# A transformer block on one core: square root on ScalarE, query projection ahead of the probabilities' transposes, band mask on small TensorE tiles

## The chip, the cores and the metric

The kernel runs on one core of a Trainium2 chip. The metric is the device time of one execution in microseconds (us). Shown are the median of several runs, and one further execution recorded by the hardware profiler. Engines: PE (TensorE, with PEld for its weight loads), DVE (VectorE), ACT (ScalarE), POOL (GpSimd), SP (queues the DMAs).

## The reference, cut to what matters

A time-mix block (RWKV style) comes first and a layer norm ends it; neither is touched. Between them lie six layers of local attention and a gated feed-forward block over 2048 tokens of 128 features, 16 heads of 64, a window of 32 and the window before it:

```
def l2norm(t): return t / max(norm(t, axis=-1), 1e-12)
q, k, v = split(shift_tokens(x) @ Wqkv, 3)          # 16 heads of 64
q = l2norm(q) * qs ; k = l2norm(k) * ksc            # then rotated by cos/sin tables
sim  = einsum(q, k of this window and the one before) * 8
sim  = where(i < j or i > j + w or no window before, -max, sim)
x = softmax(sim) @ v @ Wo + x
x = (a * gelu(gate)) @ W2 + b2 + x                  # a, gate = layernorm(shift_tokens(x)) @ W1 + b1
```

## The kernel before

Everything stays in SBUF in 32-bit floats; DMAs bring each layer's weights and spread the values `v` over window rows. The six layers of 16 token tiles (128 tokens) are 96 units of work in one software pipeline. In step `s` every engine works on several units at once: the projections and the norms of unit p = s+1, the rotated queries and keys, scores and softmax of unit a = s, and the mixing with the values and the output projection of unit b = s-1. The feed-forward part takes two tiles at a time, several steps later: odd steps hold its second half (GELU, `down`) and the start of the next norm, even steps hold `normed` and `widen`. A loop of 44 rounds, an odd step and an even step each, makes up most of the run.

The order on each engine is written out by hand in `step`, one copy per engine; engines meet only through semaphores (`wait_ge`). In the words of this document PE does in each step, in this order:

- p-transposes (L1270-1271): the probabilities of unit b, into `att`. They wait for the softmax (`weighed`) and for the last step's output in `att` having been added to the residual (`xb_ready`, DVE L1223).
- q projection (L1277-1280) into `proj_a`, k projection (L1291-1295) into `proj_b`, both of unit p.
- q-transposes of unit a (L1300, 1303), the mixing of unit b (L1308-1316, 64 products, each on a tile of 64 rows by 32 columns of the array), k-transposes of unit a (L1319-1321), o-transposes of unit b (L1323-1325).
- band and scores of unit a: two matmuls put the mask into the PSUM bank `turn` (L1331-1333), and 64 products on 64x32 tiles add the scores (L1334-1343).
- v projection of unit p (L1345-1351) into `proj_a`, once the normalized queries have been read from there (`united[0]`); in odd steps `down` and the centring of the next norm (L1354-1365), in even steps the norm's transposes (L1366-1373); the output projection of unit b (L1374-1381); in even steps `widen` (L1388-1392).

The norms of q and k: ACT squares both projections (L1054), DVE sums them (L1155), takes the root's inverse of 32 numbers per token in nine small instructions of its own (`inverse_root`, L82-105: a bit trick with `magic`, then two correction steps), and multiplies (`unite`, L1180). POOL then rotates q and k (L999, L1032, L1006; DVE does one of the products, L1233). The nine instructions hang on each other through the semaphore `rooted`. The DVE instructions ahead of them are the two halves of `divide_out` (L1161), which wait for the mixing.

ACT also copies PSUM to SBUF: `p_t`, `q_t`, `k_t`, `o_t`, `val` (the values). GELU, Exp and the other functions need table sets; a load (ACT_TABLE_LOAD) stands ahead of GELU in every odd step (L1068), and one ahead of a one-element Exp, `warm`, further down in the same step (L1093).

Of the kernel before, what the change touches and what calls it, by code (L numbers as in the profile page):

```python
# [37 lines left out]
WINDOW = 32  # L38
# [24 lines left out]
ROOT_SCALE = 3 / 8  # L63
# [15 lines left out]
ROOT_OPS = 9  # L79


def inverse_root(dve, ops, x, bound, y, work, magic, done, before):  # L82

    for i in ops:
        if i:
            dve.wait_ge(done, before + i)
        if i == 0:
            op = dve.scalar_tensor_tensor(bound, x, 1e-24, x, ALU.max, ALU.max)
        elif i == 1:
            op = dve.scalar_tensor_tensor(y.bitcast(I32), bound.bitcast(I32), -0.5, magic.bitcast(I32), ALU.mult, ALU.add)  # L90
        elif i == 2:
            op = dve.tensor_tensor(work[0], y, y, ALU.mult)
        elif i == 3:
            op = dve.tensor_tensor(work[1], work[0], bound, ALU.mult)
        elif i == 4:
            op = dve.scalar_tensor_tensor(work[0], work[1], -10.0 / 3.0, work[1], ALU.add, ALU.mult)
        elif i == 5:
            op = dve.scalar_tensor_tensor(y, work[0], 5.0, y, ALU.add, ALU.mult)
        elif i == 6:
            op = dve.scalar_tensor_tensor(work[0], y, -0.5 * ROOT_SCALE ** 2, y, ALU.mult, ALU.mult)  # L100
        elif i == 7:
            op = dve.tensor_tensor(work[1], work[0], bound, ALU.mult)
        else:
            op = dve.scalar_tensor_tensor(y, work[1], 1.5, y, ALU.add, ALU.mult)
        op.then_inc(done, 1)
# [711 lines left out]
def layers(nc, ctx, given):  # L817
# [12 lines left out]
    with ExitStack() as own:  # L830
# [8 lines left out]
        magic = sb("magic", [128, 2, HEADS])  # L839
# [4 lines left out]
        sums_min = sb("sums_min", [128, 2, HEADS])  # L844
# [27 lines left out]
        warm = sb("warm", [128, 1])  # L872

        warmed = sem("warmed")
        eps_set = sem("eps_set")
        cleared, centre_made = sem("cleared"), sem("centre_made")
# [5 lines left out]
        rooted = sem("rooted")  # L882
# [47 lines left out]
        with nc.Block() as block:  # L930
# [116 lines left out]
            def _(act):  # L1047
                def step(s, h, odd, live):
# [14 lines left out]
                    if live["down"]:  # L1063
                        act.wait_ge(down_in, (layer_of(s - 5) + 1) * 32)
                        for i, (_, size) in enumerate(CHUNKS):
                            act.wait_ge(widened, NC_ * h + i + 1)
                            after(act, gated, NC_ * h)
                            act.activation(gelu[0:size, i, :], up_out(i)[0:size, TWO:], ACT.Gelu,  # L1068
                                           bias=w_ffn[0:size, F_B1G + i:F_B1G + i + 1]).then_inc(gelued, 1)
                    if live["b"]:  # L1070
                        for j in range(2):
                            act.wait_ge(p_turned, 2 * b + j + 1)
                            after(act, mixed, 2 * b)
                            act.copy(p_t[:, 4 * j:4 * j + 4, :], bank_s[:, j, :].rearrange("p (a t) -> p a t", t=TILE))\  # L1074
                                .then_inc(p_laid, 1)
                    if live["p"]:
                        square(0)
                        square(1)
                    if live["a"]:
                        for j in range(2):  # L1080
# [3 lines left out]
                                .then_inc(q_laid, 1)  # L1084
                    if live["a"]:
# [25 lines left out]
                    if live["p"]:  # L1111
                        act.wait_ge(v_projected, 2 * p + 2)
                        after(act, v_spread, 256 * p)
                        act.copy(v_tok[mine][:, :, :, :], bank_a[:, :, :].rearrange("p a (h e) -> p a h e", e=HEAD))\  # L1114
                            .then_inc(v_laid, 1)
                    if live["a"]:
                        weigh(0)
                    if live["up"]:
# [4 lines left out]
                                       scale=w_ffn[:, F_G:F_G + 1]).then_inc(normed_f, 1)  # L1123
                    if live["a"]:
# [12 lines left out]
            def _(dve):  # L1137
# [5 lines left out]
                dve.memset(magic[:, :, :], float(np.array(0x5F3759DF, np.int32).view(np.float32))).then_inc(centre_made, 1)  # L1143
                dve.tensor_tensor(centre[:, :], identity[:, :], averager[:, :], ALU.subtract).then_inc(centre_made, 1)
                dve.wait_ge(centre_made, 2)
# [3 lines left out]
                def step(s, h, odd, live):  # L1149
                    p, a, b, mine = s + 1, s, s - 1, 1 - odd  # L1150

                    def sum_squares(j):
                        dve.wait_ge(squared[j], p + 1)
                        after(dve, rooted, ROOT_OPS * p)
# [20 lines left out]

                    def unite(j):
                        dve.wait_ge(rooted, ROOT_OPS * p + ROOT_OPS)
# [39 lines left out]
                    if live["down"]:  # L1217
                        dve.wait_ge(narrowed, h + 1)
                        dve.scalar_tensor_tensor(xa[:, columns(s - 5, 2)], bank_b[:, 1, 0:TWO], w_ffn[:, F_B2:F_B2 + 1],
                                                 xb[:, columns(s - 5, 2)], ALU.add, ALU.add).then_inc(xa_ready, 1)  # L1220
                    if live["b"]:
# [3 lines left out]
                    if live["norm"]:  # L1225
                        dve.wait_ge(dev_squared, h + 2)
                        after(dve, rstd_made, h + 1)
                        dve.tensor_reduce(var_f[:, :], dev_sq[:, :, :], AX.X, ALU.add).then_inc(var_kept, 1)
# [11 lines left out]
            def _(pe):  # L1240
                pe.wait_ge(centre_made, 2)
                mask_first, mask_other = 0, 1
# [12 lines left out]
                def step(s, h, odd, live):  # L1255
# [10 lines left out]
                    if live["b"]:  # L1266
                        pe.wait_ge(weighed, 2 * b + 2)
                        after(pe, xb_ready, b)
                        stand_alone(pe, passed)
                        for j in range(2):  # L1270
                            transposes(bank_s[:, j, :], probs_flat, j, p_turned)
                    if live["p"]:
# [7 lines left out]
                        mm.then_inc(q_projected, 1)  # L1280
                    if live["p"]:
# [44 lines left out]
                    if live["a"]:  # L1326
                        which = (mask_first if a % TILES == 0 else mask_other) if isinstance(a, int) \
                            else (tile_of(a) + 15) // 16
                        band = band_bf[:, which, :].unsqueeze(1).broadcast_to([128, PAIRS, 2 * WINDOW])
# [138 lines left out]
def position_tables():  # L1468
# [13 lines left out]
    tables = ROOT_SCALE * np.stack([both(cos * scale) * QK_SCALE, both(sin * scale) * sign * QK_SCALE,  # L1482
                                    both(cos / scale), both(sin / scale) * sign], 1)
# [6 lines left out]
def band_masks():  # L1490
# [5 lines left out]
    first = hidden | ((a < WINDOW) & (c < WINDOW))  # L1496
# [51 lines left out]
```

## Time and profile before

| | |
|---|---|
| runs | 2005.83, 2007.20, 2008.31 us; median 2007.2 us |
| profiled execution | 2001.63 us, span of its instructions 1999.8 us |
| busy share of the span | PE 89%, DVE 77%, POOL 73%, ACT 58% |
| granted TensorE clock | mean 0.975; 1.00 from 240 us to 1940 us |
| layers | from about 195 us to about 1960 us |

The profile names engine, line, operation, output and inputs of each group of instructions, the number of them, and after an arrow what ended the idle time ahead of them. A start-to-start distance on PE is more reliable than a duration, since matmuls overlap and their ends are modelled.

### The profile page before, as it was taken

The numbers are of one execution on the slowest core, as the hardware profiler recorded it, in microseconds if no ns is written. First come the engines' busy times: TensorE is split into PE (matmuls) and PEld (weight loads), VectorE is DVE, ScalarE is ACT, GpSimd is POOL, SyncE is SP. The second block draws the span as 40 slices with busy tenths as digits, with TensorE's granted clock in tenths as the row PEclk, the third lists the DMA queues.
The fourth block names the chain that finished last, engine by engine and source line by source line (L and its number), as shares of the span: only waits on it lengthen the run. The fifth ranks groups of instructions, "written<-read, shape, count | busy, mean of one in ns | idle before, by whom it ended". The sixth has DMA issues, their size and how long they took to land. (4 is left out here: it accounts for less than half of the span.)

```text
span 1999.8 us, 85355 instructions
## 1 busy us (share of the span) xinstructions
PE 1771.6 (89%) x34184; PEld 1277.4 (64%) x34184; DVE 1543.1 (77%) x2729; ACT 1156.1 (58%) x1966; POOL 1454.8 (73%) x967
## 2 busy tenths in 40 slices
PE   7764789999999999999999999999999999999995
PEld 3453466666666666666666666666666666666664
DVE  4774798778878877788788777887887788778864
ACT  2311456666666666666666666666666666666663
POOL 3221787787788778877887787778777877887771
PEclk9985899999999999999999999999999999999998
DMA  4000222223232223222223322233222232322220
GB/s 151 2 3 1 56 63 57 64 60 84 66 74 58 54 55 94 63 68 58 63 56 85 76 67 55 52 81 81 62 58 62 61 86 63 74 60 52 55 63 22
DMA packets 93581, 123.43 MB, mean 62 GB/s; under 512 B 27760, under 2 KB 41808, under 8 KB 93392
## 3 DMA queue, kind: packets, MB, share of 16 engines
q1 hardware_dynamic: 93232, 122.42, 24.3%
q8 instruction: 46, 0.75, 0.2%
q10 hardware_dynamic: 288, 0.13, 0.0%
q14 instruction: 15, 0.12, 0.0%
HBM read 20.74 MB, written 1.05 MB: 11 GB/s over the span
## 5 line engine op out<-in xcount | busy, mean ns | idle before, releaser
L999 POOL TENSOR_TENSOR across<-unit,turns 128x1024 f32<-128x1024 f32 x192 | 497.4, 2591 | 275.5 <-issue 265.6
L1006 POOL TENSOR_TENSOR rotated<-along,across 128x1024 f32<-128x1024 f32 x192 | 495.7, 2582 | 14.2
L1155 DVE TENSOR_REDUCE sums<-squares 128x16 f32<-128x1024 f32 x192 | 234.0, 1219 | 177.9 <-ACT squares L1054 177.7
L1246 PE MATMUL turn<-identity,rotated 128*128 128x128 f32 x1536 | 204.7, 276 | 35.5 <-POOL rotated L1006 34.3
L1246 PEld LDWEIGHTS turn<-identity,rotated 128*128 128x128 f32 x1536 | 172.3, 141 | 98.0 <-issue 82.5
L1032 POOL TENSOR_TENSOR along<-unit,turns 128x1024 f32<-128x1024 f32 x96 | 228.0, 2375 | 0.0
L1350 PE MATMUL proj_a<-w_qkv,shift_a 128*128 128x512 f32 x384 | 189.5, 616 | 36.3 <-DVE unit L1180 30.1
L1114 ACT COPY val<-proj_a 128x1024 f32<-128x1024 f32 x96 | 97.2, 1012 | 180.7 <-PE proj_a L1350 180.7
L1379 PE MATMUL att<-o_t,w_o 128*128 128x128 f32 x1536 | 188.9, 277 | 0.0
L1278 PE MATMUL proj_a<-w_qkv,shift_a 128*128 128x512 f32 x384 | 184.4, 603 | 5.0 <-POOL shift_a L989 3.7
L1379 PEld LDWEIGHTS att<-o_t,w_o 128*128 128x128 f32 x1536 | 181.0, 193 | 1.0 <-issue 1.0
L1089 ACT COPY k_t<-turn 128x512 f32<-128x512 f32 x192 | 103.2, 589 | 134.5 <-PE turn L1246 134.5
L1293 PE MATMUL proj_b<-w_qkv,shift_a 128*128 128x512 f32 x384 | 180.9, 593 | 0.0
L1233 DVE TENSOR_TENSOR along<-unit,turns 128x1024 f32<-128x1024 f32 x96 | 165.7, 1726 | 0.0
L1054 ACT ACTIVATE squares<-proj_a 128x1024 f32<-128x1024 f32 x96 | 98.2, 1023 | 115.8 <-PE proj_a L1278 115.8
L1312 PE MATMUL att<-v_win,p_t 64*32 64x64 f32 x12288 | 154.2, 225 | 0.8 <-ACT p_t L1074 0.8
L1338 PEld LDWEIGHTS turn<-k_t,q_t 64*32 64x32 f32 x12288 | 128.3, 105 | 41.4 <-issue 41.1
L1074 ACT COPY p_t<-att 128x512 f32<-128x512 f32 x192 | 103.1, 589 | 89.0 <-PE att L1246 89.0
L1312 PEld LDWEIGHTS att<-v_win,p_t 64*32 64x32 f32 x12288 | 135.6, 105 | 20.1 <-issue 16.9
L1161 DVE TENSOR_TENSOR heads_out<-att,inv_mass 128x512 f32<-128x512 f32 x192 | 123.6, 686 | 31.4 <-PE att L1312 31.4
L1338 PE MATMUL turn<-k_t,q_t 64*32 64x64 f32 x12288 | 144.2, 225 | 0.0
L1172 DVE TENSOR_TENSOR logits<-turn,row_max 128x512 f32<-128x512 f32 x192 | 132.8, 692 | 6.7
(201 smaller groups left out, 3366.2 us busy)
## 6 DMA issues: line engine op xcount, KB each, us to landing
v_win<-val SPq DMA_DIRECT2D x1536, 64.0 KB, 2.0
w_qkv<-wqkv_dram SPq DMA_DIRECT2D x18, 512.0 KB, 3.9
w_o<-wo_dram SPq DMA_DIRECT2D x6, 512.0 KB, 4.7
where<-positions_dram SPq DMA_DIRECT2D x1, 2048.0 KB, 10.7
w_ffn<-ffn_dram SPq DMA_DIRECT2D x12, 170.5 KB, 2.3
w_ffn<-ffn_dram SPq DMA_DIRECT2D x6, 192.0 KB, 2.3
x_tok<-x_dram SPq DMA_DIRECT2D x4, 256.0 KB, 4.2
out_dram<-final SPq DMA_DIRECT2D x4, 256.0 KB, 2.4
```

Source lines behind the costliest of these rows:

```text
L999: pool.tensor_tensor(a[:, :, ::-1, :], u, table, ALU.mult).then_inc(acrossed[j], 1)
L1006: pool.tensor_tensor(rotated[j][:, :, :], along[j][:, :, :], across[j][:, :, :], ALU.add).then_inc(rotated_in[j], 1)
L1032: pool.tensor_tensor(along[0][:, :, :], unit[0][:, :, :], turns[mine][:, 0, :].unsqueeze(1).broadcast_to([128, HEADS, HEAD]), ALU.mult).th ...
L1155: dve.tensor_reduce(sums[:, j, :], squares[j][:, :, :], AX.X, ALU.add).then_inc(summed[j], 1)
L1233: dve.tensor_tensor(along[1][:, :, :], unit[1][:, :, :], turns[mine][:, 2, :].unsqueeze(1).broadcast_to([128, HEADS, HEAD]), ALU.mult).the ...
L1246: mm = pe.transpose(bank[:, TILE * (i % 4):TILE * (i % 4) + TILE], buffer[:, TILE * i:TILE * i + TILE], identity[:, :])
L1278: mm = pe.matmul(bank_a[:, half, :], shift_a[mine][:, :], w_qkv[:, 512 * half:512 * half + 512], start=True, stop=True)
L1293: mm = pe.matmul(bank_b[:, half, :], shift_a[mine][:, :], w_qkv[:, base:base + 512], start=True, stop=True)
L1312: mm = pe.matmul(bank_s[WINDOW * w:WINDOW * w + WINDOW, par, HEAD * a_:HEAD * a_ + HEAD], p_t[rows, a_, WINDOW * w:WINDOW * w + WINDOW], v ...
L1338: mm = pe.matmul(bank_t[WINDOW * w:WINDOW * w + WINDOW, par, HEAD * a_:HEAD * a_ + HEAD], q_t[rows, a_, WINDOW * w:WINDOW * w + WINDOW], k ...
L1350: pe.matmul(bank_a[:, par, :].rearrange("p (a e) -> p a e", a=PAIRS), shift_a[mine][:, :], values[:, par, :, :], start=True, stop=True).th ...
L1379: mm = pe.matmul(bank_s[:, 0, 0:TILE], w_o[:, a_, :], o_t[:, a_, :], start=(a_ == 0), stop=(a_ == PAIRS - 1))
```

## The change

It has five parts.

1. The root moves. ACT computes `lifted = relu(sums - 1e-24)` and `root = sqrt(lifted + 1e-24)`; DVE takes the reciprocal and one Newton step (four instructions in place of nine). The table's factor 3/8, which belonged to the old steps, goes away.
2. ACT's table sets are switched by hand: the square root's set at the start of each step's work for unit p, the exponential's after the copy of `k_t`'s last window. `warm` goes.
3. PE does the q projection ahead of the p-transposes, and ACT the queries' squares ahead of the copies to `p_t`.
4. The band: eight matmuls on 64x32 tiles in place of two on the whole array. In even steps the mask comes from `band_now`, a copy that ACT makes in each even step.
5. ACT copies `val` after the first half of the softmax (and after `normed`), and DVE sums the norm's squares (`var_f`) ahead of adding to `xb`.

```diff
             def _(act):
+                    if live["p"]:
+                        act.preload_act_table_set("sqrt_and_others")
+                        square(0)
                     if live["b"]:                       # copies to p_t
...
                     if live["p"]:
-                        square(0)
                         square(1)
...
+                    if live["a"] and not odd:
+                        after(act, scored, 2 * (a - 1))
+                        act.copy(band_now[:, :], band_bf[:, which, :]).then_inc(band_set, 1)
+                    if live["p"]:
+                        act.wait_ge(summed[0], p + 1)
+                        act.wait_ge(summed[1], p + 1)
+                        after(act, rooted, 4 * p)
+                        act.activation(lifted[:, :, :], sums[:, :, :], ACT.Relu, bias=tiny[:, 0:1]).then_inc(above_tiny, 1)
+                        act.wait_ge(above_tiny, p + 1)
+                        act.activation(root[:, :, :], lifted[:, :, :], ACT.Sqrt, bias=tiny[:, 1:2]).then_inc(roots_in, 1)
...
-                    if live["down"]:
-                        after(act, warmed, h)
-                        act.activation(warm[:, :], ones[:, 0:1], ACT.Exp).then_inc(warmed, 1)
...
+                        act.preload_act_table_set("exp_and_others")
             def _(dve):
+                    def newton(square_root, x, y, work, done):
+                        dve.reciprocal(y, square_root).then_inc(rooted, 1)
+                        dve.wait_ge(rooted, done + 1)
+                        dve.scalar_tensor_tensor(work[0], y, -0.5, y, ALU.mult, ALU.mult).then_inc(rooted, 1)
+                        dve.wait_ge(rooted, done + 2)
+                        dve.scalar_tensor_tensor(work[1], x, TINY, work[0], ALU.max, ALU.mult).then_inc(rooted, 1)
+                        dve.wait_ge(rooted, done + 3)
+                        dve.scalar_tensor_tensor(y, work[1], 1.5, y, ALU.add, ALU.mult).then_inc(rooted, 1)
...
-                        dve.wait_ge(summed[0], p + 1)
-                        dve.wait_ge(summed[1], p + 1)
-                        inverse_root(dve, range(ROOT_OPS), sums[:, :, :], sums_min[:, :, :], inv_norm[:, :, :],
-                                     [w[:, :, :] for w in root_work], magic[:, :, :], rooted, ROOT_OPS * p)
+                        dve.wait_ge(roots_in, p + 1)
+                        newton(root[:, :, :], sums[:, :, :], inv_norm[:, :, :], [w[:, :, :] for w in root_work], 4 * p)
             def _(pe):
+                        if not odd:
+                            pe.wait_ge(band_set, a // 2 + 1 if isinstance(a, int) else h + 4)
                         pe.wait_ge(k_laid, 2 * a + 2)
-                        for par in range(2):
-                            pe.matmul(bank_t[:, par, :].rearrange("p (a c) -> p a c", a=PAIRS), identity_bf[:, :], band,
-                                      start=True, stop=False, skip_group_check=True)
+                        stand_alone(pe, passed)
+                        for w in range(BLOCKS):
+                            for par in range(2):
+                                rows = slice(HEAD * par, HEAD * par + HEAD)
+                                at = HEAD * par + (WINDOW if w else 0)
+                                pe.matmul(bank_t[WINDOW * w:WINDOW * w + WINDOW, par, :]
+                                          .rearrange("p (a c) -> p a c", a=PAIRS),
+                                          identity_bf[rows, at:at + WINDOW], band[rows],
+                                          start=True, stop=False, skip_group_check=True)
```

How the order moves, first on PE, in one odd step from the output projection of the step before it on (`proj_a<-w_qkv` just behind an output projection is the q projection; further down it is the v projection). Before:

```order
L1379 MATMUL att<-o_t,w_o 128x128 x8
L1246 MATMUL att<-identity,probs 128x128 x8
L1278 MATMUL proj_a<-w_qkv,shift_a0 128x512 x2
L1293 MATMUL proj_b<-w_qkv,shift_a0 128x512 x2
L1246 MATMUL turn<-identity,rotated0 128x128 x8
L1312 MATMUL att<-v_win0,p_t 32x64 x64
L1246 MATMUL turn<-identity,rotated1 128x128 x8
L1246 MATMUL att<-identity,heads_out 128x128 x8
L1332 MATMUL turn<-band_bf,identity_bf 128x512 x2
L1338 MATMUL turn<-k_t,q_t 32x64 x64
```

And with the change:

```order
L1380 MATMUL att<-o_t,w_o 128x128 x8
L1266 MATMUL proj_a<-w_qkv,shift_a0 128x512 x2
L1240 MATMUL att<-identity,probs 128x128 x8
L1287 MATMUL proj_b<-w_qkv,shift_a0 128x512 x2
L1240 MATMUL turn<-identity,rotated0 128x128 x8
L1306 MATMUL att<-v_win0,p_t 32x64 x64
L1240 MATMUL turn<-identity,rotated1 128x128 x8
L1240 MATMUL att<-identity,heads_out 128x128 x8
L1331 MATMUL turn<-band_bf,identity_bf 32x512 x8
L1339 MATMUL turn<-k_t,q_t 32x64 x64
```

Two groups have changed places (probabilities and q projection), and the band has become eight matmuls of 32 output rows.

Next ACT, over an even step from behind the copies to `q_t` to its end. Before:

```order
L1089 COPY k_t<-turn 128x4x128 x2
L1099 ACTIVATE norm_tok<-dev,rstd_f 128x128 x2
L1105 COPY o_t<-att 128x512 x2
L1109 ACTIVATE k_t<-k_t,carry_scale 128x8x32
L1114 COPY val1<-proj_a 128x1024
L1061 ACTIVATE probs<-logits 128x8x64
L1122 ACTIVATE normed<-att,w_ffn 128x256
L1061 ACTIVATE probs<-logits 128x8x64
```

With the change:

```order
L1065 COPY band_now<-band_bf 128x64
L1070 ACTIVATE lifted<-sums,tiny 128x32
L1072 ACTIVATE root<-lifted,tiny 128x32
L1077 COPY k_t<-turn 128x4x128 x2
L1084 ACTIVATE norm_tok<-dev,rstd_f 128x128 x2
L1090 COPY o_t<-att 128x512 x2
L1094 ACTIVATE k_t<-k_t,carry_scale 128x8x32
L1096 ACT_TABLE_LOAD
L1036 ACTIVATE probs<-logits 128x8x64
L1103 ACTIVATE normed<-att,w_ffn 128x256
L1108 COPY val1<-proj_a 128x1024
L1036 ACTIVATE probs<-logits 128x8x64
```

The mask's copy and the root stand ahead of the copies of the keys, a table load stands ahead of the softmax, and `val` has gone behind `normed`.

Last ACT's start of an odd step. Before:

```order
L1068 ACT_TABLE_LOAD
L1068 ACTIVATE gelu<-proj_b,w_ffn 128x256 x2
L1068 ACTIVATE gelu<-turn,w_ffn 85x256
L1074 COPY p_t<-att 128x512 x2
L1054 ACTIVATE squares0<-proj_a 128x1024
L1054 ACTIVATE squares1<-proj_b 128x1024
```

With the change:

```order
L1043 ACT_TABLE_LOAD
L1043 ACTIVATE gelu<-proj_b,w_ffn 128x256 x2
L1043 ACTIVATE gelu<-turn,w_ffn 85x256
L1046 ACT_TABLE_LOAD
L1029 ACTIVATE squares0<-proj_a 128x1024
L1052 COPY p_t<-att 128x512 x2
L1029 ACTIVATE squares1<-proj_b 128x1024
```

A second load follows GELU, and the queries' squares stand ahead of the copies to `p_t`. Per odd and even step together there are five loads, where there were two.

## Rows read from the trace of the kernel before

**Rows 1.** Busy time by engine in the steady stretch, from the windows view.

```profile
600.00:1800.00 1200.00, 1116.77 (x21714) 813.65 (x21705) 965.28 (x1672) 759.72 (x1283) 964.30 (x623) 1.00 0.27 66
```

**Rows 2.** PE's timeline, one odd-even round: start, us, engine, line, operation, count, [idle before].

```profile
1002.45 1.96 PE L1350 MATMUL proj_a<-w_qkv,shift_a 128*128 128x512 f32 x4 [0.49 <-DVE unit L1180]
...
1008.56 1.06 PE L1246 MATMUL att<-identity,probs 128*128 128x128 f32 x8 [0.62 <-issue]
1009.46 1.88 PE L1278 MATMUL proj_a<-w_qkv,shift_a 128*128 128x512 f32 x4
...
1016.03 1.09 PE L1246 MATMUL turn<-identity,rotated 128*128 128x128 f32 x8 [0.58 <-POOL rotated L1006]
1016.98 1.09 PE L1246 MATMUL att<-identity,heads_out 128*128 128x128 f32 x8
1018.04 0.60 PE L1332 MATMUL turn<-band_bf,identity_bf 128*128 x2
1018.57 1.48 PE L1338 MATMUL turn<-k_t,q_t 64*32 64x64 f32 x128
1020.28 1.96 PE L1350 MATMUL proj_a<-w_qkv,shift_a 128*128 128x512 f32 x4 [0.23 <-DVE unit L1180]
...
1024.40 1.99 PE L1262 MATMUL proj_b<-normed,w_ffn 128*128 128x256 f32 x8 [0.16 <-ACT normed L1122]
...
1032.37 1.62 PE L1312 MATMUL att<-v_win,p_t 64*32 64x64 f32 x128
...
1035.53 1.09 PE L1246 MATMUL att<-identity,heads_out 128*128 128x128 f32 x8 [0.51 <-DVE heads_out L1161]
```

**Rows 3.** The timeline again, VectorE alone, in the same round.

```profile
1008.16 0.29 DVE L1223 TENSOR_TENSOR xb<-att,xa 128x128 f32 x1 [1.65 <-PE att L1379]
...
1014.15 1.22 DVE L1155 TENSOR_REDUCE sums<-squares 128x16 f32<-128x1024 f32 x1 [0.41 <-ACT squares L1054]
...
1015.64 1.29 DVE L1161 TENSOR_TENSOR heads_out<-att,inv_mass 128x512 f32<-128x512 f32 x2 [0.27 <-PE att L1312]
...
1016.84 0.18 DVE L88 SCALAR_TENSOR_TENSOR sums_min<-sums 128x32 f32<-128x32 f32 x1
...
1018.73 0.19 DVE L104 SCALAR_TENSOR_TENSOR inv_norm<-root_work,inv_norm 128x32 f32<-128x32 f32 x1
1018.96 1.22 DVE L1180 TENSOR_TENSOR unit<-proj_a,inv_norm 128x1024 f32<-128x1024 f32 x1
```

**Rows 4.** Groups of the steady stretch: line, engine, operation, count | busy, mean ns | idle before.

```profile
L1191 DVE RECIPROCAL inv_mass<-mass 128x16 f32<-128x16 f32 x66 | 16.7, 253 | 2.3
...
L1093 ACT ACTIVATE warm<-ones 128x1 f32<-128x1 f32 x32 | 6.5, 203 | 0.4
L1068 ACT ACT_TABLE_LOAD x33 | 42.3, 1283 | 0.6
```

**Rows 5.** The timeline, ScalarE alone, in the same round.

```profile
1009.22 1.07 ACT L1074 COPY p_t<-att 128x512 f32<-128x512 f32 x2 [1.90 <-PE att L1246]
...
1016.72 1.07 ACT L1089 COPY k_t<-turn 128x512 f32<-128x512 f32 x2 [1.64 <-PE turn L1246]
1017.68 0.70 ACT L1099 ACTIVATE norm_tok<-dev,rstd_f 128x128 f32<-128x128 f32 x2
...
1024.24 0.63 ACT L1061 ACTIVATE probs<-logits 128x512 f32<-128x512 f32 x1
1024.88 1.28 ACT L1068 ACT_TABLE_LOAD   x1
1026.18 0.84 ACT L1068 ACTIVATE gelu<-proj_b,w_ffn 128x256 f32<-128x256 f32 x2
```

**Rows 6.** The timeline, POOL alone: from the first rotation of an odd step on.

```profile
1002.48 2.35 POOL L999 TENSOR_TENSOR across<-unit,turns 128x1024 f32<-128x1024 f32 x1 [2.79 <-issue]
...
1009.56 3.34 POOL L999 TENSOR_TENSOR across<-unit,turns 128x1024 f32<-128x1024 f32 x1
...
1013.54 2.36 POOL L1006 TENSOR_TENSOR rotated<-along,across 128x1024 f32<-128x1024 f32 x1
```

More of the change, by code:

```diff
@@ L75, in stand_alone @@
     engine.sem_inc(passed, 1)
[L79 to L105, printed above, removed]
+TINY = 1e-24
 def tile_of(n):
@@ L843, in layers @@
         sums = sb("sums", [128, 2, HEADS])
-        sums_min = sb("sums_min", [128, 2, HEADS])
+        lifted = sb("lifted", [128, 2, HEADS])
+        root = sb("root", [128, 2, HEADS])
+        tiny = sb("tiny", [128, 2])
         inv_norm = sb("inv_norm", [128, 2, HEADS])
@@ L871, in layers @@
         hidden = sb("hidden", [128, NC_, TWO])
-        warm = sb("warm", [128, 1])
-        warmed = sem("warmed")
         eps_set = sem("eps_set")
+        band_now = sb("band_now", [128, 2 * WINDOW], BF16)
+        band_set = sem("band_set")
         cleared, centre_made = sem("cleared"), sem("centre_made")
@@ L1123, in step @@
                                        scale=w_ffn[:, F_G:F_G + 1]).then_inc(normed_f, 1)
+                    if live["p"]:
+                        act.wait_ge(v_projected, 2 * p + 2)
+                        after(act, v_spread, 256 * p)
+                        act.copy(v_tok[mine][:, :, :, :], bank_a[:, :, :].rearrange("p a (h e) -> p a h e", e=HEAD))\
+                            .then_inc(v_laid, 1)
                     if live["a"]:
@@ L1220, in step @@
                                                  xb[:, columns(s - 5, 2)], ALU.add, ALU.add).then_inc(xa_ready, 1)
+                    if live["norm"]:
+                        dve.wait_ge(dev_squared, h + 2)
+                        after(dve, rstd_made, h + 1)
+                        dve.tensor_reduce(var_f[:, :], dev_sq[:, :, :], AX.X, ALU.add).then_inc(var_kept, 1)
                     if live["b"]:
@@ L1264, in widen @@
                         mm.then_inc(widened, 1)
[L1266 to L1271, printed above, removed]
                     if live["p"]:
@@ L1280, in step @@
                         mm.then_inc(q_projected, 1)
+                    if live["b"]:
+                        pe.wait_ge(weighed, 2 * b + 2)
+                        after(pe, xb_ready, b)
+                        stand_alone(pe, passed)
+                        for j in range(2):
+                            transposes(bank_s[:, j, :], probs_flat, j, p_turned)
                     if live["p"]:
@@ L1326, in step @@
                     if live["a"]:
-                        which = (mask_first if a % TILES == 0 else mask_other) if isinstance(a, int) \
-                            else (tile_of(a) + 15) // 16
-                        band = band_bf[:, which, :].unsqueeze(1).broadcast_to([128, PAIRS, 2 * WINDOW])
+                        band = (band_bf[:, mask_other, :] if odd else band_now[:, :]).unsqueeze(1)\
+                            .broadcast_to([128, PAIRS, 2 * WINDOW])
+                        if not odd:
+                            pe.wait_ge(band_set, a // 2 + 1 if isinstance(a, int) else h + 4)
                         pe.wait_ge(k_laid, 2 * a + 2)
-                        for par in range(2):
-                            pe.matmul(bank_t[:, par, :].rearrange("p (a c) -> p a c", a=PAIRS), identity_bf[:, :], band,
-                                      start=True, stop=False, skip_group_check=True)
+                        stand_alone(pe, passed)
+                        for w in range(BLOCKS):
[6 more added lines that the diff above has]
+                                          start=True, stop=False, skip_group_check=True)
                         for a_ in range(PAIRS):
@@ L1495, in band_masks @@
     hidden = (c - WINDOW > i) | (i > c)
-    first = hidden | ((a < WINDOW) & (c < WINDOW))
+    first = hidden | ((a % (2 * WINDOW) < WINDOW) & (c < WINDOW))
     return np.stack([first, hidden], 1).astype(np.float32) * np.float32(MASKED_BIT)
```

32 lines of the change are left out of this document (12 added, 20 removed).

## The prediction

> **What bounds the kernel now.** I read the windows first, then PE's timeline of one round, then the other engines at the places where PE waits. In the steady stretch PE is busy for 1116.8 of 1200 us, DVE for 965, POOL for 964 and ACT for 760 [rows 1]; the stretch holds 33 GELU table loads [rows 4], one per pair of steps, so a pair takes 1200/33 = 36.4 us and PE leaves about 2.5 us of it idle. PE's timeline shows where [rows 2]. In the odd step the v projection waits 0.49 us for the normalized queries; at the start of the even step the p-transposes wait 0.62 us, put down to "issue", while DVE adds to `xb` just before them (1008.16 to 1008.45) [rows 3], which is what their semaphore asks for. In the even step the k-transposes wait 0.58 for POOL, the v projection 0.23, `widen` 0.16; in the odd step the o-transposes wait 0.51 for DVE's `heads_out`. The sum is 2.59 us, the whole idle time. So PE's fixed order sets the pace, and its waits are short ends of chains on other engines.
>
> One of these chains closes a loop of its own. From the odd step's normalized queries POOL runs without idle from 1002.48 to 1015.90 [rows 6]; 0.13 us later the k-transposes start [rows 2]. From there PE runs through to the odd step's mixing at 1032.37, and then `heads_out`, the root and `unit` follow on DVE, which is where the loop began. A saving counts fully only if it lies in this loop too.
>
> **The root on DVE.** Nine instructions now take 1018.96 - 1016.84 = 2.12 us [rows 3]. In their place stand a reciprocal and three dependent ones. The last of the old ones starts 0.23 us ahead of `unit` [rows 3], so three make 0.69. A reciprocal of 16 numbers per partition takes 253 ns [rows 4]; for 32 it costs 0.25 if the length didn't matter and 0.51 if it doubled; I take 0.35, since a small DVE instruction takes 0.18 to 0.19 whatever it does [rows 3]. Sum 1.05 with the hand-over, so `unit` comes 1.05 us earlier (bounds 0.9 and 1.2), if the root is there in time. Both v-projection waits, 0.49 and 0.23, are shorter than that and go.
>
> **The root on ACT.** Relu and Sqrt of 32 numbers: the one-element Exp took 203 ns [rows 4], a 128-element one 0.35 (two in 0.70) [rows 5]; I take 0.25 each and 0.2 for hand-overs, 0.7 together (bounds 0.5 and 1.0). They can start when the second sum ends (1014.15 + 1.22 = 1015.37) and are wanted when `heads_out` ends (1015.64 + 1.29 = 1016.93) [rows 3]. That covers 1.56 us. ACT idles there too: 1.64 us before the copies to `k_t` [rows 5]. Cost nothing; if the cover goes (the sums late by more than 0.8), the root pushes `unit`.
>
> **The table loads.** Three more per pair at 1.283 us [rows 4]. The two for the root come after `dev` in one step, where ACT idles 1.90 before `p_t` [rows 5], and after GELU in the other, where the squares behind it wait for the q projection. The two for Exp come behind the carry copy. The softmax there waits for DVE's scores, which come after `unit`, now about 1 us earlier; the load just fits. `normed` no longer stands behind `val` (1 us); so `widen`'s 0.16 goes. One ACT pair is then 760/33 = 23.0, less the 0.2 of `warm`, plus 3.85 of loads, 1.0 of roots and 0.25 for `band_now`: 27.9 us of 34.7, with room.
>
> What a load costs beside its own 1.283 us is open to argument, because five switches hang on it. Here it starts at 1024.88, when the softmax ends (1024.24 + 0.63), and GELU begins 0.02 us after its end [rows 5]; 33 of them had 0.6 us idle ahead in all [rows 4]. So I charge 1.30. The Trainium skill (ScalarE: Activation LUTs, section "What ACT_TABLE_LOAD costs") counts a drain of some 1380 ns to every switch beside the same 1283, about 2.66 us, and advises against alternating sets. By it the pair would be longer than now (third rival); this trace does not show that drain.
>
> **q projection first.** The 0.62 us wait is covered by a projection of 1.72 to 1.88 us [rows 2] that needs nothing from DVE's addition: its input, and the free bank once `val` is copied. `val` moves behind the softmax's first half, but the v projection is earlier by up to 0.49; I see it copied some 2 us before PE asks. What waits instead is `p_t`, later by one projection less the gap; ACT copies it behind the squares and ends some 1 us before the mixing. `heads_out` depends on the mixing alone. Saved: 0.62.
>
> **The band.** Today two matmuls of 512 columns take 1018.57 - 1018.04 = 0.53 us, 0.26 each [rows 2]. Eight small ones are new. The scores' 128 records on the same 64x32 tiles take 1.48 us, 11.6 ns apart [rows 2], though each moves an eighth of 512 columns; tiles plainly run side by side. If all eight do, the band takes one stream and seven pitches, 0.26 + 0.08 = 0.34, saving 0.19 per step. Bounds: 0.10 (eight pitches, hidden under the scores) and 8 x 0.26 = 2.1 (one after the other). I take 0.34, the nearest row being the scores' own. `band_now` is made 2 us before it is asked for. `var_f` moves ahead of `xb` at no cost: PE's output projection ends only later.
>
> **What stays.** The k-transposes' 0.58 and the o-transposes' 0.51 are not touched: `heads_out` still takes 0.27 + 1.29 + 0.1 after the mixing, against 0.95 us of k-transposes. When POOL is on time, that becomes a wait of 0.5 to 0.7 in each step.
>
> **The sum.** By PE's order, per pair: 0.49 + 0.23 + 0.62 + 0.16 + 2 x 0.19 = 1.88 us. By the loop through POOL: 1.05 (root) + 0.23 + 0.16 + 0.19 (one band) = 1.63 us. The longer loop is left, so the smaller saving decides, near 1.7, as POOL's part also holds an instruction of 3.34 us against 2.35 for its like [rows 6], lengthened by DVE beside it, which can shift either way. There are 96 steps, 48 pairs; the first and the last are not in this rhythm, so 47: 1.7 x 47 = 80 us. The profiled execution took 2001.6 us, so 1921.6; the runs' median is 5.6 above it, and gives 2007.2 - 80 = **1927 us**.
>
> **Rivals.** *The bands run one after another* (slower): 2.1 in place of 0.53 adds 1.57 per step; PE's order then is 3.1 - 1.5 = 1.6 per pair longer, 2007.2 + 1.6 x 47 = 2083 us. It turns into a loss when the band takes over 1.3 us, that is when fewer than two tiles overlap. For it: the band is new in this form and every column tile reads the same rows. Against it: the scores' pitch. 5%.
>
> *ScalarE late with the root*: if Relu, Sqrt and their hand-overs take 1.6 us or more, or stand behind a late copy, `unit` comes only 0.3 earlier than now; the pair saves 0.8, not 1.7: 2007.2 - 38 = 1969 us. For it: five instructions more in ACT's strict order. Against: the 1.56 us of cover. 8%.
>
> *Each switch costs twice its load* (slower): five times another 1.3 make ACT's pair 34.3 us. In the odd step the chain from the softmax's end through load, GELU (1.3), load, squares (1.0) and `p_t` (1.07) then takes 8.5 us, where PE reaches the mixing 1032.37 - 1024.87 = 7.5 after it [rows 2, 5], and now has no wait. The mixing is 1.0 to 1.4 late, the k projection, which waits for the gated GELU, 0.7, the o-transposes and `normed` another 0.6 each; with the even step's 0.5 the pair is 3.5 longer than forecast, 1.8 longer than now: 2007.2 + 85 = 2092 us. This is the skill's rule of the section named above. Against: the rows show nothing behind 33 loads. 5%.
>
> **How the numbers follow.** The forecast has 80%, the rivals 5, 8 and 5, and 2% is left for what I don't see. Within the forecast the best is the band at 0.10 and POOL's lengthened instruction gone: the loop then saves 1.05 + 0.23 + 0.16 + 0.43 + 0.99 = 2.86, PE's order 1.50 + 0.86 = 2.36, so 2.36 x 47 = 111 and 1896 us. The worst is no gain from the band and a reciprocal of 0.51: 0.9 + 0.39 = 1.29, 61 us, 1946. With the late root the upper end is about 1970. Range 1893 to 1970. A measurement of this kernel can tell about 0.2%, 4 us, from no change. Faster by more than that: forecast, late root and 1% of the rest less what a still later root would take, 87%; within it 3%; slower 10% (the two slow rivals).
>
> **What would show it.** Right: in the steady stretch a pair near 34.7 us; the v projection, `widen` and the transposes of the probabilities without waits; the waits of k- and o-transposes left at 0.5 to 0.7; ACT near 28 us per pair, five loads of 1.28 with nothing behind them; four root instructions in 1.05 us and no DVE wait for ACT's `root`; band to scores 0.34 apart. Wrong: PE waiting for `p_t` at the mixing or for the gated GELU at the k projection (loads dearer); a DVE wait for `root` ahead of the reciprocal (late root); a start-to-start of band and scores above 1 us.

## The result and the profile after

The changed kernel takes 1974.6 us (median of 4 runs, 1971.8 to 1980.3) against 2006.5: ratio 0.984, 95% interval 0.982 to 0.987. That is 32 us faster where 80 were forecast, above the range's upper end. The profiled execution took 1973.1 us, with a span of 1971.3.

PE's timeline of the changed kernel, with the columns of [rows 2], shows what became of the waits:

```profile
1006.27 1.09 PE L1240 MATMUL turn<-identity,rotated 128*128 128x128 f32 x8 [0.89 <-POOL rotated L979]
...
1008.16 0.41 PE L1331 MATMUL turn<-band_now,identity_bf 64*32 64x512 bf16 x8
1008.39 1.46 PE L1339 MATMUL turn<-k_t,q_t 64*32 64x64 f32 x128
1009.86 1.95 PE L1351 MATMUL proj_a<-w_qkv,shift_a 128*128 128x512 f32 x4
...
1013.65 1.89 PE L1256 MATMUL proj_b<-normed,w_ffn 128*128 128x256 f32 x8
...
1017.97 1.04 PE L1240 MATMUL att<-identity,probs 128*128 128x128 f32 x8
1020.39 1.96 PE L1287 MATMUL proj_b<-w_qkv,shift_a 128*128 128x512 f32 x4 [1.39 <-DVE hidden L1192]
...
1026.25 1.09 PE L1240 MATMUL att<-identity,heads_out 128*128 128x128 f32 x8 [0.34 <-DVE heads_out L1148]
...
1028.96 1.96 PE L1351 MATMUL proj_a<-w_qkv,shift_a 128*128 128x512 f32 x4
...
1036.01 1.04 PE L1240 MATMUL att<-identity,probs 128*128 128x128 f32 x8
...
1042.06 1.09 PE L1240 MATMUL turn<-identity,rotated 128*128 128x128 f32 x8 [0.89 <-POOL rotated L979]
```

The four waits that the forecast removed (0.49, 0.62, 0.23 and 0.16 of [rows 2]) are gone. The band is as hoped or better: 0.23 us from its start to that of the scores, 0.53 before. But PE waits 0.89 + 1.39 + 0.34 = 2.62 us per pair, as much as the 2.59 before. A new wait of 1.39 us, the odd step's k projection for the gated GELU, has taken the place of the old ones. The pair takes 1042.06 - 1006.27 = 35.79 us against 36.4. In a count of PE's own work that is the two bands' 2 x 0.30, but this doesn't make them the cause: with the old bands put back (x_old_band below) the pair takes 35.82, as the waits shrink in their place. So PE's own work does not set the pair here.

The chain behind it, from DVE's and POOL's timelines of the same round:

```profile
1008.07 1.22 DVE L1176 TENSOR_TENSOR unit<-proj_a,inv_norm 128x1024 f32<-128x1024 f32 x1
...
1014.04 0.29 DVE L1221 TENSOR_TENSOR xb<-att,xa 128x128 f32 x1 [0.98 <-PE att L1380]
1014.25 3.35 DVE L1227 TENSOR_TENSOR along<-unit,turns 128x1024 f32<-128x1024 f32 x1
1017.53 1.21 DVE L1183 TENSOR_REDUCE mass<-probs 128x16 f32<-128x1024 f32 x1
...
1018.99 0.87 DVE L1192 SCALAR_TENSOR_TENSOR hidden<-proj_b,w_ffn,gelu 128x256 f32<-128x256 f32 x2
1019.78 0.47 DVE L1192 SCALAR_TENSOR_TENSOR hidden<-turn,w_ffn,gelu 85x256 f32<-85x256 f32 x1
...
1026.11 0.34 DVE L1164 RECIPROCAL inv_norm<-root 128x32 f32<-128x32 f32 x1
...
1027.17 1.22 DVE L1176 TENSOR_TENSOR unit<-proj_a,inv_norm 128x1024 f32<-128x1024 f32 x1
...
1014.17 2.35 POOL L979 TENSOR_TENSOR rotated<-along,across 128x1024 f32<-128x1024 f32 x1
1016.48 3.34 POOL L972 TENSOR_TENSOR across<-unit,turns 128x1024 f32<-128x1024 f32 x1
```

The timelines of the kernel before, in the same place:

```profile
1024.47 0.29 DVE L1223 TENSOR_TENSOR xb<-att,xa 128x128 f32 x1 [0.51 <-PE att L1379]
1024.68 1.40 DVE L1233 TENSOR_TENSOR along<-unit,turns 128x1024 f32<-128x1024 f32 x1
...
1022.63 2.36 POOL L1032 TENSOR_TENSOR along<-unit,turns 128x1024 f32<-128x1024 f32 x1
1025.07 3.23 POOL L1006 TENSOR_TENSOR rotated<-along,across 128x1024 f32<-128x1024 f32 x1
```

`along` takes 3.35 us in place of 1.40. Read the two engines side by side: POOL's `rotated` begins at 1014.17, DVE's `along` 0.08 later, and `along` ends 1.08 us after `rotated` does (1016.52); POOL's next instruction is then the longer one. Before, `along` began 0.39 ahead of `rotated`, and `rotated` was stretched. The 1.40 us hold a wait too: POOL's own product, also named `along` (L1032), ran until 1024.99, and DVE's ended 1.09 us after that. From 600 to 1800 us DVE's `along` always begins beside a POOL instruction, and in all of them, 66 before and 67 with the change, it ends 1.07 to 1.09 us after that one's end. The two products don't run side by side; the one that starts first holds the other back. All else on DVE is in a row behind `along`: the softmax's sum, its reciprocal and three gated products, the third of which ends at 1020.25, and PE's k projection starts at 1020.39.

ScalarE, which two rivals blamed, does not hold this up, as its timeline at that place shows:

```profile
1013.66 0.64 ACT L1036 ACTIVATE probs<-logits 128x512 f32<-128x512 f32 x1
1014.31 1.28 ACT L1043 ACT_TABLE_LOAD   x1
1015.61 0.84 ACT L1043 ACTIVATE gelu<-proj_b,w_ffn 128x256 f32<-128x256 f32 x2
1016.45 0.47 ACT L1043 ACTIVATE gelu<-turn,w_ffn 85x256 f32<-85x256 f32 x1
1016.94 1.28 ACT L1046 ACT_TABLE_LOAD   x1
1018.24 1.02 ACT L1029 ACTIVATE squares<-proj_a 128x1024 f32<-128x1024 f32 x1
```

GELU ends at 1016.92, 2.9 us before DVE's last gated product begins; each of these loads is followed by work 0.02 us after its end.

### The profile page after: what moved, and what is told of

It is laid out like the page before. It is cut to its first block and busy times, and to the rows that moved or that the text cites. A ratio compares the mean times of both kernels' runs of the same rounds, so it can differ in the third digit from the quotient of the medians.

```text
span 1971.3 us, 86246 instructions
## 1 busy us (share of the span) xinstructions
PE 1741.7 (88%) x34760; PEld 1282.0 (65%) x34760; DVE 1529.1 (78%) x2250; ACT 1392.7 (71%) x2301; POOL 1457.7 (74%) x967
## 3 DMA queue, kind: packets, MB, share of 16 engines
HBM read 20.74 MB, written 1.05 MB: 11 GB/s over the span
## 5 line engine op out<-in xcount | busy, mean ns | idle before, releaser
L972 POOL TENSOR_TENSOR across<-unit,turns 128x1024 f32<-128x1024 f32 x192 | 541.1, 2818 | 237.2 <-issue 226.5
L979 POOL TENSOR_TENSOR rotated<-along,across 128x1024 f32<-128x1024 f32 x192 | 454.7, 2368 | 15.2 <-DVE along L1227 1.2
L1227 DVE TENSOR_TENSOR along<-unit,turns 128x1024 f32<-128x1024 f32 x96 | 235.8, 2457 | 0.0
L1029 ACT ACTIVATE squares<-proj_b 128x1024 f32<-128x1024 f32 x96 | 98.6, 1027 | 118.0 <-PE proj_b L1287 118.0
L1306 PE MATMUL att<-v_win,p_t 64*32 64x64 f32 x12288 | 161.5, 226 | 6.2 <-issue 5.3
L1306 PEld LDWEIGHTS att<-v_win,p_t 64*32 64x32 f32 x12288 | 141.9, 105 | 26.4 <-issue 23.1
L1339 PEld LDWEIGHTS turn<-k_t,q_t 64*32 64x32 f32 x12288 | 140.7, 105 | 9.7 <-issue 4.6
L1287 PEld LDWEIGHTS proj_b<-w_qkv,shift_a 128*128 128x128 f32 x384 | 65.7, 190 | 110.0 <-issue 109.9
L1156 DVE TENSOR_REDUCE row_max<-turn 128x8 f32<-128x512 f32 x192 | 130.5, 680 | 8.6 <-PE turn L1339 8.6
```

What stands on the lines that cost most here:

```text
L972: pool.tensor_tensor(a[:, :, ::-1, :], u, table, ALU.mult).then_inc(acrossed[j], 1)
L979: pool.tensor_tensor(rotated[j][:, :, :], along[j][:, :, :], across[j][:, :, :], ALU.add).then_inc(rotated_in[j], 1)
L1029: act.activation(squares[j][:, :, :], by_head((bank_a, bank_b)[j]), ACT.Square)\
L1227: dve.tensor_tensor(along[1][:, :, :], unit[1][:, :, :], turns[mine][:, 2, :].unsqueeze(1).broadcast_to([128, HEADS, HEAD]), ALU.mult).the ...
L1287: mm = pe.matmul(bank_b[:, half, :], shift_a[mine][:, :], w_qkv[:, base:base + 512], start=True, stop=True)
L1306: mm = pe.matmul(bank_s[WINDOW * w:WINDOW * w + WINDOW, par, HEAD * a_:HEAD * a_ + HEAD], p_t[rows, a_, WINDOW * w:WINDOW * w + WINDOW], v ...
```

## Experiments

Three theories are told apart. A: DVE's `along` and POOL's instructions exclude each other, and which of them starts first decides. B: ScalarE is late through its loads and the root. C: the loop through POOL holds the pair anyway.

**x_along_first**: `along` ahead of the addition to `xb` in even steps.

```diff
+                    if live["p"] and not odd:
+                        along_k()
                     if live["b"]:
                         dve.wait_ge(attended, b + 1)
                         dve.tensor_tensor(xb[:, columns(b)], ...
-                    if live["p"]:
+                    if live["p"] and odd:
+                        along_k()
```

> The changed kernel with one edit: in even steps DVE does its product for the keys' rotation (along) ahead of the addition to xb. Theory A (the two-input product on DVE and POOL's instruction exclude each other; in the even step POOL's rotated began 0.08 us before along, so along took 3.35 us, and the softmax's sum, the gated GELU and the odd step's k projection came late): along falls to about 2.3 us or less, the k projection's wait of 1.39 goes, the pair falls from 35.7 to 34.4-34.8 us, time 1915 to 1935 us. Theory B (ScalarE is late through its loads and the root): the 1.39 stays, time 1965 to 1980. Theory C (the loop through POOL holds the pair anyway): the 1.39 goes, but the wait of the k-transposes grows by about as much, pair 35.4 or more, time 1955 to 1975.

Measured: 1910.3 us, ratio 0.952 (0.948 to 0.956). From its timelines of DVE, POOL and PE:

```profile
1024.40 2.20 DVE L1223 TENSOR_TENSOR along<-unit,turns 128x1024 f32<-128x1024 f32 x1
...
1023.15 2.37 POOL L1005 TENSOR_TENSOR along<-unit,turns 128x1024 f32<-128x1024 f32 x1
1025.60 3.22 POOL L979 TENSOR_TENSOR rotated<-along,across 128x1024 f32<-128x1024 f32 x1
...
1017.69 1.09 PE L1245 MATMUL turn<-identity,rotated 128*128 128x128 f32 x8 [0.88 <-POOL rotated L979]
...
1030.26 1.88 PE L1292 MATMUL proj_b<-w_qkv,shift_a 128*128 128x512 f32 x4
...
1036.06 1.09 PE L1245 MATMUL att<-identity,heads_out 128*128 128x128 f32 x8 [0.54 <-DVE heads_out L1148]
```

POOL's `rotated` is now the stretched one. `along` takes 2.20 us, since it waits for the end of POOL's instruction before (1025.52) and ends 1.08 after it. The k projection follows without a wait. One moved instruction gives 64 us more than the change, and this kernel is faster than both. The length of `along` and the vanished wait are as A said; the time is 5 us below A's range, and the pair, 34.17 us, a little below it too. B falls, since ScalarE's loads and root are untouched and the wait is gone. C falls as the reason for this loss, since the k-transposes wait no longer than in the changed kernel (0.88 and 0.89).

**x_one_input**: a probe with `along` as a one-input instruction. It leaves out the multiplication by the position table, so its output is not the block's.

```diff
-                        dve.tensor_tensor(along[1][:, :, :], unit[1][:, :, :], <table>, ALU.mult)
+                        dve.tensor_reduce(along[1][:, :, :], unit[1][:, :, :].unsqueeze(3), AX.X, ALU.add)
```

> A probe: the changed kernel, with DVE's product for the keys' rotation replaced by a one-input instruction of the same size (a sum over an axis of length 1), so the multiplication by the position table is left out for that half of the keys. Theory A: it takes about 1.2 us in both steps whatever POOL does, POOL's second across falls from 3.34 to 2.35 us, the k projection's wait of 1.39 goes, the pair is 34.2 to 34.6 us, time 1905 to 1925 us. Theory B: the k projection still waits over 1 us, time above 1960. Theory C: the gain comes from POOL's shorter chain, the wait of the k-transposes falls from 0.89 towards 0, the time lies between 1930 and 1955.

Measured: 1900.2 us, 0.947 (0.945 to 0.950), faster than A's range. From its timelines of DVE and POOL:

```profile
1023.98 1.21 DVE L1227 TENSOR_REDUCE along<-unit 128x1024 f32<-128x1024 f32 x1
...
1023.89 2.37 POOL L979 TENSOR_TENSOR rotated<-along,across 128x1024 f32<-128x1024 f32 x1
1026.20 2.36 POOL L972 TENSOR_TENSOR across<-unit,turns 128x1024 f32<-128x1024 f32 x1
```

It starts 0.09 us after `rotated`, as in the changed kernel, and neither is stretched. So DVE's work as such does not exclude POOL's instruction. The probe changes the operation as well as the number of inputs, but the changed kernel has a DVE product with one of its two inputs in PSUM: `unit` from `proj_b` takes 1.21 us from 1028.31 on, and POOL's `across`, which begins at 1028.53, its usual 2.35. What the excluding form has, and these two have not, is two inputs in SBUF. The time doesn't measure the exclusion alone: POOL's chain is shorter too, and the k-transposes' wait of 0.89 is gone, as C expected of it.

**x_old_root**: the changed kernel with the nine instructions, without ScalarE's root and with two table loads per pair. **y_along_old_root**: the same with `along` first.

```diff
-                        dve.wait_ge(roots_in, p + 1)
-                        newton(root[:, :, :], ...
+                        inverse_root(dve, range(ROOT_OPS), ...
```

> The changed kernel with the old root (nine DVE instructions, no root on ScalarE, two table loads per pair). Theory A: unit and so POOL come 1.1 us later, along on DVE then starts ahead of POOL's rotated in the even step, as before the change, takes about 1.4 us, and the k projection does not wait; what comes back are the v projection's waits (0.2 to 0.5). Pair 35.0 to 35.5 us, time 1940 to 1965 us: the root's move was no gain in this order. Theory B says the same sign, because ScalarE has three loads less, and also that along would stay above 3 us. Additive parts (each part gains by itself): slower than the changed kernel, 1990 to 2005 us.

> x_along_first (the product along ahead of xb in even steps) with the old root on DVE and no root on ScalarE. Theory A: with the old root DVE began along ahead of POOL's rotated anyway (x_old_root: 1.39 us), so this edit brings nothing there: pair 35.6 to 35.8 us, time 1972 to 1985 us, and the root's move is worth some 65 to 70 us once along goes first. If along-first gains by itself, whoever holds the port: 1915 to 1950 us.

Measured: 1980.0 us, 0.987 (0.985 to 0.990), and 1983.2 us, 0.989 (0.986 to 0.992). From x_old_root's timelines of DVE, POOL and PE, and below them DVE's `along` of y_along_old_root:

```profile
1024.44 1.39 DVE L1241 TENSOR_TENSOR along<-unit,turns 128x1024 f32<-128x1024 f32 x1
...
1024.83 3.22 POOL L1007 TENSOR_TENSOR rotated<-along,across 128x1024 f32<-128x1024 f32 x1
...
1016.02 1.09 PE L1254 MATMUL turn<-identity,rotated 128*128 128x128 f32 x8 [1.18 <-POOL rotated L1007]
```

```profile
1026.10 2.18 DVE L1237 TENSOR_TENSOR along<-unit,turns 128x1024 f32<-128x1024 f32 x1
```

As A said, the old root leaves `along` ahead of `rotated` and the k projection without a wait, and the edit of x_along_first then brings nothing: `along` begins earlier, and waits for POOL. My time for x_old_root (1940 to 1965) was too low: beside the two waits of the v projection that I expected (0.45 and 0.64), POOL, 1.1 us later, now holds the k-transposes for 1.18 us, which I had left out. So in the changed order the root's move is worth 5 us, within the intervals; with `along` first it is worth 1983 - 1910 = 73.

**x_old_band** and **y_along_old_band**: two matmuls on the whole array again, without and with `along` first.

```diff
-                        for w in range(BLOCKS):
-                            for par in range(2):
-                                pe.matmul(<32 rows>, identity_bf[rows, at:at + WINDOW], band[rows], ...
+                        for par in range(2):
+                            pe.matmul(<128 rows>, identity_bf[:, :], band, ...
```

> The changed kernel with the band as before, two matmuls on the whole array. The start-to-start of band and scores goes from 0.23 back to 0.53 us. If PE's order sets the pace in both steps (A): 0.6 us per pair more, 1998 to 2006 us, no gain left. If POOL's loop sets it (C): 0.3 per pair, 1985 to 1992 us. If the band was hidden: 1970 to 1978 us.

> x_along_first with the band as before. The loop through POOL (pair 34.2: the k-transposes of the even step wait 0.88 us for it) holds the even step's band and not the odd step's: 0.3 us per pair more, 1920 to 1928 us. If PE's order alone sets the pace: 0.6 per pair, 1934 to 1942. If the band is still hidden: 1906 to 1914.

Measured: 1978.1 us (0.986, 0.983 to 0.989) and 1915.5 us (0.955, 0.952 to 0.959). The new band is worth some 4 us without and 5 with `along` first, less than any expectation but "hidden" (both times lie just above its ranges), and the differences lie within the intervals. In x_old_band most of the 0.3 us per step is given back at the waits: the k projection waits 1.12 in place of 1.39 and the k-transposes 0.66 in place of 0.89, and the pair is 1041.64 - 1005.82 = 35.82 us.

**x_old_q** and **y_along_old_q**: the p-transposes ahead of the q projection again, and the copies to `p_t` ahead of the queries' squares, without and with `along` first.

```diff
+                    if live["b"]:
+                        transposes(...)            # probabilities
                     if live["p"]:
                         pe.matmul(bank_a[:, half, :], ...
-                    if live["b"]:
-                        transposes(...)            # probabilities
```

> The changed kernel, along still behind xb, with the p-transposes ahead of the q projection again on PE and ScalarE. In the even step the wait for xb (about 0.6 us) and in the odd step nothing new: the k projection waits for the gated GELU there whatever stands first. Theory A (the odd step is held by DVE's late product): xb's wait shows in the even step and costs 0.4 to 0.6 us per pair, 1992 to 2004 us, unless it shifts along ahead of POOL's rotated, which would show as along near 1.4 to 2.3 us in the even step and a time below 1970 us.

> x_along_first with the p-transposes ahead of the q projection again, on PE and on ScalarE. By the loop through POOL: the wait for xb comes back at the start of the even step, 0.5 to 0.6 us, but lies beside POOL's chain, where PE waits 0.88 anyway; 0 to 0.1 us per pair, 1906 to 1918 us. By PE's order, as the prediction counted it: 0.6 per pair, 1935 to 1943 us.

Measured: 2003.4 us, 1.000 (0.998 to 1.002), and 1935.3 us, 0.966 (0.963 to 0.969). x_old_q keeps the late `along` beside the returned wait, as its timelines of PE and DVE show:

```profile
1009.85 1.07 PE L1240 MATMUL att<-identity,probs 128*128 128x128 f32 x8 [0.62 <-issue]
...
1031.55 1.96 PE L1287 MATMUL proj_b<-w_qkv,shift_a 128*128 128x512 f32 x4 [1.38 <-DVE hidden L1192]
...
1025.42 3.33 DVE L1227 TENSOR_TENSOR along<-unit,turns 128x1024 f32<-128x1024 f32 x1
```

The q projection is worth 29 us (2003 to 1975) and 25 us. For the second my expectation by POOL's loop (1906 to 1918 us) failed; PE's order (1935 to 1943) was right. With the wait for `xb` back ahead of it, the mixing of the even step starts 7.87 us after the output projection, against 7.07 in x_along_first, and `heads_out` moves with it: the k-transposes no longer wait for POOL, but the o-transposes wait 0.33 there as well. How much of the 25 us each part makes is not shown.

**z_rstd_late**: x_along_first, and POOL's `rstd` behind the end of the keys' rotation. **z_rstd_late_again** is the same kernel; its profile is the one read.

```diff
-                    if live["norm"]:
-                        pool.tensor_tensor(rstd_f[:, :], ...
                     if live["p"]:
                         add_turned(1, p)
+                    if live["norm"]:
+                        pool.tensor_tensor(rstd_f[:, :], ...
```

> x_along_first with one more edit on POOL: the norm's rstd (0.70 us, odd steps) goes behind the addition that ends the keys' rotation. If the loop through POOL sets the pair: that chain is 0.70 shorter, the k-transposes' wait falls from 0.88 to about 0.2, the o-transposes' wait of about 0.35 to 0.5 appears in the even step as well, and the pair falls by 0.25 to 0.35 us to about 33.9, as in x_one_input; time 1893 to 1900 us. If it isn't the loop: 1906 to 1914.

> The kernel of z_rstd_late again, for a profile of an undisturbed execution: time 1893 to 1903 us; pair about 33.9 us; the k-transposes of the even step wait 0.3 us or less, the o-transposes 0.3 to 0.55 in both steps.

Measured: 1899.3 us (0.947, 0.944 to 0.951) and 1902.2 us (0.950, 0.948 to 0.953). From z_rstd_late_again's timeline of PE:

```profile
1009.24 1.09 PE L1245 MATMUL turn<-identity,rotated 128*128 128x128 f32 x8 [0.39 <-POOL rotated L979]
...
1027.98 1.09 PE L1245 MATMUL att<-identity,heads_out 128*128 128x128 f32 x8 [0.56 <-DVE heads_out L1148]
```

The wait for POOL falls from 0.88 to 0.39, where 0.3 or less was expected, and the time lies within the range. So after x_along_first the loop through POOL does hold the even step in part; the gain over x_along_first (about 8 to 11 us) is at the edge of the intervals.

**z_mix_first**: on top, the mixing ahead of the q-transposes.

```diff
+                    if live["b"]:
+                        for a_ in range(PAIRS): ...          # mixing
                     if live["a"]:
                         transposes(bank_t[:, 0, :], rotated_flat[0], 0, q_turned)
...
-                    if live["b"]:
-                        for a_ in range(PAIRS): ...          # mixing
```

> z_rstd_late with the mixing ahead of the q-transposes on PE, so that heads_out on DVE has two groups of transposes beside it. If the o-transposes' wait for heads_out (about 0.5 us and the exposed tail of the matmul before it, in each step) is what is left: that wait goes, a smaller one of the k-transposes for the copies to q_t (0.2 to 0.4) comes, pair 33.4 to 33.7 us, time 1875 to 1892 us. If the copies to q_t are later than I think: 1895 to 1910 us.

Measured: 1908.6 us, 0.954 (0.951 to 0.957): the hoped-for gain is missed, the kernel is slower than z_rstd_late, and the time lies in the second range. From its timeline of PE, and below it from its list of waits (us in total, times, longest):

```profile
1013.51 1.09 PE L1245 MATMUL turn<-identity,rotated 128*128 128x128 f32 x8 [0.29 <-ACT q_t L1060]
```

```profile
DVE inv_norm L1164 <- ACT root L1072: 40.1, 70, 0.8
```

The o-transposes' wait goes, but the k-transposes wait for ScalarE's later copies to `q_t` (and between 600 and 1800 us 23 times still for POOL), and DVE, done earlier with `heads_out`, now waits 40.1/70 = 0.57 us per step for ScalarE's root: the wait that the late-root rival described. What each of these costs is not shown.

## Why the prediction was wrong

- **Direction** and the four removed waits were right: both v projections, the p-transposes and `widen` run without one. The waits that were to stay at 0.5 to 0.7 did not: the k-transposes wait 0.89, the o-transposes 0.34 and only in the odd step.
- **Root on DVE**, forecast 1.05 us with a reciprocal of 0.35: it takes 0.34, and the four take 1027.17 - 1026.11 = 1.06. The reason given for the 0.35 was weaker than that: of the old nine, L92 takes 0.29 on average, not the "0.18 to 0.19 whatever it does" that the two rows shown suggested. **Root on ScalarE**: forecast 0.25 per instruction, measured 0.32, from the groups of the steady stretch:

```profile
L1096 ACT ACT_TABLE_LOAD x68 | 87.2, 1283 | 1.2
...
L1046 ACT ACT_TABLE_LOAD x67 | 86.0, 1283 | 1.2
...
L1072 ACT ACTIVATE root<-lifted,tiny 128x32 f32<-128x32 f32 x67 | 21.5, 321 | 2.2
```

  It stayed beside `heads_out`; the late-root rival's time, 1969, comes near the measured one by accident, as DVE does not wait for it here.
- **Table loads**: 1.283 us each with 1.2 us of idle ahead of 67 of them, 0.02 each. The charge of 1.30 held, and the rule of the Trainium skill (ScalarE: Activation LUTs, section "What ACT_TABLE_LOAD costs") of a drain beside it isn't seen in this kernel.
- **Band**: forecast 0.34, measured 0.23. It was mis-sized to the good, but in time it is worth 4 to 5 us, where the sum counted 0.19 to 0.38 per pair, 9 to 18 us.
- **The failed step** is in "The sum" and, ahead of it, in the sentence on POOL's instruction of 3.34 us [rows 6], "lengthened by DVE beside it, which can shift either way". I read the stretch on POOL's side alone and left `along` at its old length. But `unit`, and POOL behind it, comes earlier by more than `along`, which stands behind `xb` and the output projection. Counted from the even step's k-transposes, `unit` starts 1.13 us earlier (1.80 us after them, before 2.93) and `xb` 0.67 (7.77, before 8.44). That moves `rotated` from 0.39 us behind `along` to 0.08 ahead of it. `along` grows by 1.95, and behind it wait the softmax's sum, the gated GELU and the k projection, which waits 1.39. The sum had no term for that chain.
- A sign of being wrong did show, under another cause: the prediction named the k projection's wait for the gated GELU, and put "loads dearer" beside it. The loads are not dearer; the wait comes through `along`, and none of the rivals named that.
- With that one instruction out of the way the time comes near the forecast: x_along_first takes 95 us less than the kernel before, where 80 were forecast. That is in part luck, since the terms don't hold one by one: beside it the band is worth 5 us, the root 73 where 1.05 x 47 = 49 were counted, and the q projection 25 although it lies outside POOL's loop, to which the sum had given the last word.

The Trainium skill (SBUF — State Buffer, section "Who interferes with whom") says that a DVE instruction with two inputs in SBUF contends with a GpSimd instruction that reads SBUF, calls the port pair that they share an exclusive lock, and adds: "Issue order, not op shape, decides who blocks." The rows agree: 1.40 against 3.35 us for the same `along`, 1.21 for the one-input probe beside POOL.

## What to carry to other kernels

When an edit makes one engine earlier, list again which long instructions of DVE (those with two inputs in SBUF) and POOL start next to each other, and who starts first: here half a microsecond of order was worth 64 us. Look at what is queued behind the one that may lose, not at its own wait. A wait that is removed counts only after the next one in the fixed order has been put in its place: the same root was worth some 5 us or 73, depending on one neighbour.

## What the runs showed that was not expected

- A wait on PE can cost more than its idle time in the timeline. With the wait, the p-transposes of y_along_old_q start 2.57 us after the output projection; without one, in x_along_first, the q projection starts 1.79 us after it. PE's timelines of the two, y_along_old_q first:

```profile
1007.35 1.95 PE L1385 MATMUL att<-o_t,w_o 128*128 128x128 f32 x16
1009.92 1.06 PE L1245 MATMUL att<-identity,probs 128*128 128x128 f32 x8 [0.62 <-issue]
```

```profile
1008.14 1.95 PE L1385 MATMUL att<-o_t,w_o 128*128 128x128 f32 x16
1009.93 1.88 PE L1271 MATMUL proj_a<-w_qkv,shift_a 128*128 128x512 f32 x4
```

  That is 0.78 us for a listed wait of 0.62; the other 0.16 us, I take it, is the end of the last matmul, which otherwise lies under the next one. It is not the same everywhere: from the scores to the v projection it is 1.71 us before, with a listed wait of 0.23, and 1.47 with the change, without one, so there the list holds all but 0.01.
- When DVE's product has waited for a POOL instruction, it gets in before POOL's next one, which is ready at once: in the changed kernel `along` ends 1.08 us after `rotated`, and `across` is longer by 0.99 (3.34 against 2.35).
- Eight 64x32 matmuls of 512 columns span 0.41 us, and the scores on the same tiles start 0.23 us after the first of them: they need not wait for all eight.
